# The first bias of the routed experts moves from a matmul into a row of the weights, with two raw buffers, fewer waits between the adds and 24 result slots

## What is computed

```python
x = x + tanh(g_xattn[0]) * xattn(_layernorm(x), ctx_1024, ctx_1024, Wq, bq, Wk, bk, Wv, bv, Wo, bo)
x = x + tanh(g_ffn[0]) * ffn(_layernorm(x), gate_w, gate_b, sw1, sb1, sw2, sb2, rw1, rb1, rw2, rb2)

def ffn(x, ...):                      # D = 256, FFN = 256, 8 experts, 1 shared, top 2
    hs = einsum('bsd,ndf->nbsf', x, sw1) + sb1[:, None, None, :]
    shared_out = einsum('nbsf,nfd->bsd', swiglu(hs), sw2) + sb2.sum(0)
    probs = softmax(x @ gate_w + gate_b, axis=-1)
    topk_probs, topk_idx = top_k(probs, 2)
    cw = sum(one_hot(topk_idx, 8) * topk_probs[..., None], axis=2)
    hr = einsum('bsd,edf->ebsf', x, rw1) + rb1[:, None, None, :]
    out_e = einsum('ebsf,efd->ebsd', swiglu(hr), rw2) + rb2[:, None, None, :]
    return shared_out + einsum('ebsd,bse->bsd', out_e, cw)
```

## Time and profile before

| | |
|---|---|
| runs | 696.72, 694.03, 694.46 us |
| median | 694.46 us |
| the profiled execution | 697.65 us |
| its span | 695.8 us |
| PE busy | 635.5 us (91%) |
| DVE busy | 482.7 us (69%) |
| ACT busy | 424.3 us (61%) |
| POOL busy | 230.7 us (33%) |
| mean granted clock of PE | 0.969 |

### The profile page before, as it was taken

The page is one execution under the profiler, slowest core; times in us unless marked ns, Lnnn a source line. Parts: engine busy times, 40 slices in busy tenths (PEclk is TensorE's granted clock), DMA queues, the critical chain, the costliest instruction groups (busy, mean ns, idle before and its releaser), DMA issues.

```text
span 695.8 us, 12724 instructions
## 1 busy us (share of the span) xinstructions
PE 635.5 (91%) x3603; PEld 332.6 (48%) x3616; DVE 482.7 (69%) x805; ACT 424.3 (61%) x842; POOL 230.7 (33%) x243
## 2 busy tenths in 40 slices
PE   3997687999999999999999999999988989999990
PEld 3776561223333333333333333345456778888870
DVE  4785879778888888888888888847777844444430
ACT  4674344777777777777777777766734224444440
POOL 2343324303431442244100211220057804555552
PEclk9998897999999999999999999999999999999995
DMA  7999697964697689767843660224079665655445
GB/s 238 333 270 310 222 233 176 154 97 95 143 192 197 187 157 186 193 172 153 163 62 61 90 106 32 92 75 168 24 266 312 231 184 87 102 98 96 73 47 143
DMA packets 82820, 108.22 MB, mean 156 GB/s; under 512 B 16553, under 2 KB 64563, under 8 KB 81814
## 3 DMA queue, kind: packets, MB, share of 16 engines
q1 hardware_dynamic: 71912, 78.58, 49.0%
q0 software_dynamic: 10864, 29.10, 15.8%
HBM read 62.10 MB, written 47.35 MB: 157 GB/s over the span
## 4 chain that ended last, share of the span: by engine, by line
PE 65%; issue 13%; POOL 6%; DVE 6%; DMA 5%; SPq 2%; ACT 1%; POOLq 1%; ACTq 0%; DVEq 0%
PE psS L1492 16%; PE psO L1519 16%; PE psM L1474 14%; PE psH L1737 8%; PE psY L1763 3%; POOL zs L720 3%; DMA kq<-k_parts 2%; DVE mneg L1125 1%; PE psO L1416 1%; DVE mneg L1049 1%; PE psX L1725 1%; PE psH L1748 1%; DMA acc<-ysb,ids 1%; PE psF L1446 1%; POOL parts L614 1%
## 5 line engine op out<-in xcount | busy, mean ns | idle before, releaser
L1125 DVE TENSOR_REDUCE mneg<-psM 128x1 f32<-128x1024 f32 x240 | 282.6, 1219 | 60.7 <-PE psM L1474 60.7
L859 ACT ACTIVATE pr<-psS 128x512 f32<-128x512 f32 x488 | 266.7, 595 | 94.8 <-PE psS L1492 94.8
L1492 PE MATMUL psS<-kq 99*128 99x512 bf16 x488 | 152.4, 385 | 2.1 <-DMA kq<-msb 1.5
L1519 PE MATMUL psO<-pr,vt 128*32 128x512 f32 x1024 | 136.4, 605 | 0.0
L1474 PE MATMUL psM<-kq 96*128 96x512 bf16 x480 | 127.3, 386 | 4.8 <-DVE mneg L1125 3.1
L1492 PEld LDWEIGHTS psS<-kq 99*128 99x128 bf16 x488 | 39.8, 97 | 149.6 <-ACT pr L859 131.3
L766 POOL DMA_INDIRECT acc<-ysb,ids x39 | 60.2, 1543 | 66.9 <-ACT ysb L982 32.1
L600 POOL TENSOR_TENSOR msb<-mcp,none 16x128 bf16<-16x128 f32 x16 | 6.2, 389 | 224.7 <-ACT mcp L836 224.7
L1474 PEld LDWEIGHTS psM<-kq 96*128 96x128 bf16 x480 | 46.2, 98 | 63.4 <-DVE mneg L1125 9.1
L1737 PE MATMUL psH<-wall,zgT 128*128 x234 | 68.2, 427 | 0.9 <-DVE zgT L1357 0.9
L1363 DVE TENSOR_TENSOR rg<-psH,rs 128x256 f32<-128x256 f32 x39 | 16.5, 424 | 66.4 <-ACT rs L970 66.4
(11 more groups left out here) (246 smaller groups left out, 828.5 us busy)
## 6 DMA issues: line engine op xcount, KB each, us to landing
kq<-k_parts SPq DMA_DIRECT2D x96, 128.0 KB, 5.7
w_parts<-wraw POOLq DMA_DIRECT2D x14, 768.0 KB, 4.3
wall<-w_parts SPq DMA_DIRECT2D x7, 1536.0 KB, 7.8
v_pad<-vst SPq DMA_DIRECT2D x16, 512.0 KB, 8.7
vt<-v_pad SPq DMA_DIRECT2D x16, 512.0 KB, 7.9
wraw<-wexp POOLq DMA_DIRECT2D x9, 768.0 KB, 7.6
k_parts<-parts SPq DMA_DIRECT2D x16, 384.0 KB, 6.7
kq<-q_parts SPq DMA_DIRECT2D x96, 64.0 KB, 5.3
```

Source lines behind the costliest of these rows:

```text
L859: nc.scalar.activation(pr[:, slot, j], score_bank(s, j), ACT.Exp, scale=SCALE).then_inc(e_done, 1)
L1125: V.tensor_reduce(mneg[:, parity, i:i + 1], psM[:, i % 2], X_AXIS, ALU.max, negate=True).then_inc(m_free, 1)
L1492: mm(score_bank(s, j), kst[:, slot, j, kt * P:(kt + 1) * P], qst[:, slot, j], start=True, stop=True).then_inc(s_full, 1)
L1519: last = mm(psO[j * VW:(j + 1) * VW, u % 2], vt[:, u, k, j * VW:(j + 1) * VW], pr[:, k % 4, j], start=(k == 0), stop=(k == KT - 1), skip_g ...
```

## The change

The change uses that a normalised row has the sum 0. The last number of a row is minus the sum of the others, so from each row of `w1` the last row can be subtracted and the last number of the row is then free. POOL writes 1.0 there before the scatter, and the last row of `w1` is replaced by the expert's first bias.

- **PE:** `tile_first` has six matmuls in place of seven. `brow1`, its clearing on POOL and its two loads on SP are gone, and so are the three parts of the first bias: SP stores the bias once, as fp32 rows (`b1_rows`), and POOL cuts only the second bias into parts.
- **POOL in attention:** `last_row_in` loads the last row of `w1` into all partitions of `aT` (a broadcast of 512 numbers). `less_last_row` starts the load of the bias into partition 127, subtracts the last row from both halves of `w1` (128 x 512, and 127 x 512), and waits for that load. This is done for seven late experts and the last routed one, 8 times in all.
- **Two raw buffers:** the raw weights of the late experts lie in `wraw[:, 0]` and the new `raw2` by turns. `raw_in(e + 1)` now comes at the end of `stage(e)`; the wait for the stores is in front of the cast.
- **POOL in the scatter:** a memset of 128 x 4 numbers and a wait ahead of each of the four batches.
- **Adds:** no wait at every sixth add; only the first of an expert's run waits. `ysb` has 24 slots, and ACT waits, from tile 24 on, for the issue of the add 8 before its own. DVE's table loses one instruction (L1290), POOL two iotas.

```diff
@@ -61,9 +61,8 @@
 TILES_R = NB * NQ * 2 // P + NR - 1
 TAB = 40
 ZG = 11
-YB = 12
-DRAIN = 6
-LAST_DRAIN = 30
+YB = 24
+RUN = NQ * NB // P
 WCOLS = DT * 2 * FF + DT * D
 BLK = 512
 EPS = 1e-5
...
@@ -144,9 +142,12 @@
         sZ = ExitStack()
         ysb = sb("ysb", [P, YB, D], F32, sZ)
         sb("shift", [P, QT * D + 2 * 2 * DT * BLK + DT * D + DT * BLK - YB * D + 4], F32, sZ)
-        brow1 = sb("brow1", [P, NE, 2 * D], BF16, sZ)
         brow2 = sb("brow2", [P, NE, D], BF16, sZ)
         sZ.close()
+        sR = ExitStack()
+        sb("raw_shift", [P, QT * D], F32, sR)
+        raw2 = sb("raw2", [P, WCOLS], F32, sR)
+        sR.close()
         a_in, zT0, wo_s, aT, zT1, zT2, zx012, pt, small, cmp, rank, chosen, before, held, uone, slf, slot_f, slot_u, nt2, tok, spare = (
             sb(*a) for a in z_names)
...
@@ -479,9 +481,10 @@
                 sp.wait_ge(o_taken, 4 * b + u + 2)
                 sp.dma_start(attn[b, :, :, u * HG * DH:(u + 1) * HG * DH], ast[:, u % 2]).then_inc(a_st[u % 2], 16)
-            sp.wait_ge(bp_ok, 2)
+            sp.wait_ge(bt_ok, 1)
+            sp.dma_start(b1_rows.rearrange("e (m p) -> (e m) p", p=P), b1_t[:]).then_inc(b1_st, 16)
+            sp.wait_ge(bp_ok, 1)
             for s in range(3):
-                sp.dma_start(b1_parts[s].rearrange("(q p) -> q p", p=P), b1_p[:, s]).then_inc(bp_st, 16)
                 sp.dma_start(b2_parts[s].rearrange("(e d) -> e d", d=D), b2_p[:, s]).then_inc(bp_st, 16)
             with sp.Fori(0, NB - 1) as b:
...
@@ -537,10 +540,7 @@
                     sp.dma_start(zs[bass.ds(row, P)], fill).then_inc(fill_st, 16)
             store_base(0)
-            sp.wait_ge(brow_ok, 2)
-            b1_rows = b1_parts.rearrange("s (e c) -> s e c", e=NE)
-            sp.dma_start(brow1[0:3, 0:NR], b1_rows[:, 1:NE]).then_inc(brow_ld, 16)
-            sp.dma_start(brow1[0:3, NR:NE], b1_rows[:, 0:1]).then_inc(brow_ld, 16)
+            sp.wait_ge(brow_ok, 1)
             sp.dma_start(brow2[0:3], b2_parts.rearrange("s (e c) -> s e c", e=NE)).then_inc(brow_ld, 16)
             store_base(1)
...
@@ -668,6 +666,28 @@
                                         ALU.add).then_inc(xb_ok, 1)
+            def raw_at(e):
+                return raw2[:] if e % 2 else wraw[:, 0]
+            def last_row_at(nth):
+                return aT[:, nth % 2]
+            def last_row_in(nth, e):
+                nc.gpsimd.dma_start(last_row_at(nth), wexp[raw_of(e), P - 1:P, 2 * FF:4 * FF].to_broadcast([P, 2 * FF])).then_inc(last_ld, 16)
+            def less_last_row(nth, e, raw):
+                if nth == 0:
+                    pool.wait_ge(b1_st, 16)
+                nc.gpsimd.dma_start(raw[P - 1:P, 2 * FF:4 * FF], b1_rows[raw_of(e):raw_of(e) + 1]).then_inc(b1_ld, 16)
+                pool.wait_ge(last_ld, 16 * (nth + 1))
+                nc.gpsimd.tensor_tensor(raw[:, 0:2 * FF], raw[:, 0:2 * FF], last_row_at(nth), ALU.subtract).then_inc(less_ok, 1)
+                nc.gpsimd.tensor_tensor(raw[0:P - 1, 2 * FF:4 * FF], raw[0:P - 1, 2 * FF:4 * FF], last_row_at(nth)[0:P - 1],
+                                        ALU.subtract).then_inc(less_ok, 1)
+                pool.wait_ge(less_ok, 2 * nth + 2)
+                pool.wait_ge(b1_ld, 16 * (nth + 1))
             def prepare(nth, e, r):
                 hi, lo = (wall[:, w_at(e) + 12 * part:w_at(e) + 12 * (part + 1)].rearrange("p u c -> p (u c)")
@@ -679,24 +699,29 @@
             def stage(e):
+                raw, hi = raw_at(e), wraw[:, 1]
                 pool.wait_ge(raw_ld[0], 16 * (2 + e))
-                nc.gpsimd.tensor_copy(wraw[:, 1].bitcast(F32R), wraw[:, 0]).then_inc(wp_hi, 1)
+                less_last_row(1 + e, e, raw)
+                if e:
+                    pool.wait_ge(wp_st, 32 * e)
+                nc.gpsimd.tensor_copy(hi.bitcast(F32R), raw).then_inc(wp_hi, 1)
                 pool.wait_ge(wp_hi, e + 1)
-                nc.gpsimd.tensor_tensor(wraw[:, 0].bitcast(F32R), wraw[:, 0], wraw[:, 1], ALU.subtract).then_inc(wp_ok, 1)
+                nc.gpsimd.tensor_tensor(raw.bitcast(F32R), raw, hi, ALU.subtract).then_inc(wp_ok, 1)
                 pool.wait_ge(wp_ok, e + 1)
-                nc.gpsimd.dma_start(w_parts[e, :, 0:WCOLS], wraw[:, 1]).then_inc(wp_st, 16)
-                nc.gpsimd.dma_start(w_parts[e, :, WCOLS:2 * WCOLS], wraw[:, 0]).then_inc(wp_st, 16)
+                nc.gpsimd.dma_start(w_parts[e, :, 0:WCOLS], hi).then_inc(wp_st, 16)
+                nc.gpsimd.dma_start(w_parts[e, :, WCOLS:2 * WCOLS], raw).then_inc(wp_st, 16)
+                if e + 1 < LATE:
+                    raw_in(e + 1)
             def raw_in(e):
-                pool.wait_ge(wp_st, 32 * e)
-                nc.gpsimd.dma_start(wraw[:, 0], wexp[raw_of(e)]).then_inc(raw_ld[0], 16)
+                nc.gpsimd.dma_start(raw_at(e), wexp[raw_of(e)]).then_inc(raw_ld[0], 16)
+                last_row_in(1 + e, e)
             for n in range(UNITS - 1):
                 if n >= UNITS - NG:
                     bias_x(n - UNITS + NG)
-                if 3 <= n < 2 + LATE:
-                    raw_in(n - 2)
                 split_max(n + 1, (n + 1) % 2)
                 if n == EARLY:
                     load_tail()
@@ -705,6 +730,10 @@
                 if n < EARLY:
                     pool.wait_ge(raw_ld[n], 16)
+                    if n == 0:
+                        last_row_in(0, NE - 2)
+                    else:
+                        less_last_row(0, NE - 2, wraw[:, 1])
                     prepare(n, NE - 1 - n, n)
                     if n == 1:
                         raw_in(0)
@@ -715,6 +744,8 @@
             def scatter(b):
                 pool.wait_ge(sl_ok, b + 1)
+                nc.gpsimd.memset(zx(b)[:, :, D - 1:D], 1.0).then_inc(ones_z, 1)
+                pool.wait_ge(ones_z, b + 1)
                 for k in range(2):
                     for t in range(QT):
                         nc.gpsimd.indirect_dma_start(
@@ -738,16 +769,13 @@
             nc.gpsimd.iota(row_i[:, 0:16], pattern=[[P, 16]], base=0, channel_multiplier=0).then_inc(io_c, 1)
             nc.gpsimd.iota(row_i[:, 16:16 + TAB], pattern=[[1, TAB]], base=0, channel_multiplier=0).then_inc(io_c, 1)
             nc.gpsimd.iota(row_i[:, 16 + TAB:64], pattern=[[REGION, NR]], base=0, channel_multiplier=0).then_inc(io_c, 1)
-            nc.gpsimd.iota(row_i[:, 64:64 + LAST_DRAIN + DRAIN], pattern=[[DRAIN, LAST_DRAIN // DRAIN + 1], [0, DRAIN]], base=0, channel_multiplier=0).then_inc(io_c, 1)
-            nc.gpsimd.iota(row_i[:, 64 + LAST_DRAIN + DRAIN:], pattern=[[0, TAB + 2 - LAST_DRAIN - DRAIN]], base=LAST_DRAIN, channel_multiplier=0).then_inc(io_c, 1)
-            pool.wait_ge(io_c, 9)
+            pool.wait_ge(io_c, 7)
             nc.gpsimd.tensor_copy(rowc[:], row_i).then_inc(u_ok, 1)
             scatter(2)
             scatter(3)
             pool.wait_ge(h_full, 6)
             pool.wait_ge(sc_done, 16 * 2 * QT * (NB - 1))
-            nc.gpsimd.memset(brow1[:].rearrange("p e c -> p (e c)").bitcast(F32), 0.0).then_inc(brow_ok, 1)
             nc.gpsimd.memset(brow2[:].rearrange("p e c -> p (e c)").bitcast(F32), 0.0).then_inc(brow_ok, 1)
             pool.wait_ge(base_st, 16 * NB)
@@ -757,12 +785,7 @@
                     waits = add_waits(mybir.EngineType.Pool, T_WAIT + i, 4)
                 pool.wait_ge(ry_ok, i + 1)
                 pool.wait_ge(id_ok, i + 1)
-                if i % DRAIN == 0 and i <= LAST_DRAIN:
-
-                    pool.wait_ge(added, 16 * (i + 1))
-                else:
-
-                    pool.wait_ge(added, waits[i % 4])
+                pool.wait_ge(added, waits[i % 4])
                 nc.gpsimd.indirect_dma_start(
                     out=acc[:, :], out_offset=bass.IndirectOffsetOnAxis(ap=ids[:, i:i + 1], axis=0),
                     in_=ysb[:, i % YB], in_offset=None, bounds_check=NB * NQ + (1 + SPARES) * P - 1, compute_op=ALU.add,
@@ -978,7 +1001,7 @@
                 act.wait_ge(ry_full, i + 1)
                 if i >= YB:
-                    act.wait_ge(issued, DRAIN * ((i - DRAIN) // DRAIN) + 1)
+                    act.wait_ge(issued, i - YB + RUN + 1)
                 nc.scalar.activation(ysb[:, i % YB], psQ[:, i % 2, 0:D], ACT.Identity,
                                      scale=zg[:, i % ZG, bass.ds(e + D, 1)]).then_inc(ry_ok, 1)
...
@@ -1287,7 +1310,6 @@
                 V.scalar_tensor_tensor(out=tab[:, T_W:T_W + TAB], in0=e_f, scalar=float(WU), in1=at,
                                        op0=ALU.mult, op1=ALU.add).then_inc(tab_ok, 1)
                 link(V.scalar_tensor_tensor(out=gone, in0=e_f, scalar=NR - 0.5, in1=gone, op0=ALU.is_lt, op1=ALU.mult))
-                link(V.tensor_tensor(gone, gone, drained, ALU.max))
                 V.tensor_scalar(tab[:, T_WAIT:T_WAIT + TAB], gone, 1.0, 16.0, ALU.add, ALU.mult).then_inc(tab_ok, 1)
             beside_attention = {1: ((r_sum, 0), (r_scale, 0)), 3: ((r_sum, 1), (r_scale, 1)), 5: ((r_sum, 2),), 6: ((r_low, 0), (r_scale, 2)),
```

(5 more changed lines are left out.)

34 lines of the change are left out of this document (16 added, 18 removed).

## The result

| | kernel before | kernel after |
|---|---|---|
| runs | 696.72, 694.03, 694.46, 690.95 us | 710.17, 712.44, 716.19, 706.86 us |
| median | 694.25 us | 711.31 us |
| the profiled execution | 697.65 us | 710.17 us |
| its span | 695.8 us | 708.3 us |
| mean granted clock of PE | 0.969 | 0.956 |

The ratio is 1.022, its 95% interval 1.0148 to 1.0292. The forecast was 685.4 us, in a range of 683 to 689.5. The change made the kernel 1.5 to 2.9% slower.

A forecast was written before the change was run, and what follows sets the result against it. PE's matmuls were taken to bound attention units and the tile stage. The terms -8.5 (bias matmul) + 0 (adds) + 0 (POOL in attention) - 0.6 (before first tile) = -9.1 us gave a median of 685.4 us, range 683 to 689.5.

The forecast's parts named there:

- POOL in attention: Staging of late experts: new subtractions, DMA issues and wait take 5.2 of POOL's 14.8 us idle per unit; cost 0.
- Rival D: Attention: split_max comes late in seven staging units because POOL waits for a landing, PE stops; 698 us, chance 0.05.
- The matmul of the bias: Tile stage: removing one 512-column matmul per tile gives 0.235 us each, 8.5 us over 36 first layers.
- Rival A: Tile stage: the first fp32 weight load shows, leaving 0.145 us gained per tile; median 688.6 us, chance 0.10.
- Adds and slots: Tile stage: dropping waits between adds, with 24 slots, gives 0 itself but avoids the last add being at least 2.3 us late.
- rival C: Tile stage: POOL's adds set the pace, run starts cost more than 4.69 us; 2 or 3 us back, median 688, chance 0.05.
- Between scatter and first tile: Stretch before the tiles: a 2.04 us memset goes, four small ones with waits come at 0.3 each; net -0.6 us.
- Rival B: Scatter: batches wait far longer than 0.3 us for memsets or land late, tile stage begins late; 689.0 us, chance 0.07.

The follow-up runs named there:

- the repeated pair: Kernel before and kernel after run again unchanged, each with its own new profile: 695.57 us (one run) and 711.15 us, ratio 1.0206.
- e4: Kernel before without the first-bias matmul in each tile, keeping the old waits at every sixth add and 12 slots: 706.02 us, ratio 0.9937 to the kernel before.
- e1: Kernel after with the last row of w1 loaded into one partition instead of broadcast to 128: 709.04 us, ratio 0.9999 to the kernel before.
- the first job: First of three batches of follow-up runs, holding e1, e2, e3 and e4; the kernel before had a median of 708.8 us in it.
- e3: Kernel after without last row, bias row, subtractions and their waits; two raw buffers and new tile stage stay: 693.09 us, ratio 0.9782 to the kernel before.
- e2: Kernel after without the load of the bias row and POOL's wait for it: 698.95 us, ratio 0.9846 to the kernel before.

## Why the prediction was wrong

**The step that failed** is "POOL in attention", with its "Cost 0; its upper end is 0 as well unless a DMA takes 10 us longer". It cost 24 us (26.6 in the repeated pair, where 2.8 are unit 2's). The step counted POOL's idle time, and there it was right: the new work fits, and POOL still waits 9.0 to 13.7 us for the maxima in each staging unit. It left out, without a reason, what the moved and added DMAs do to the transfers of the other engines: POOL's stores, 1.5 MB a unit, moved from 7.1 to 14.7 us of a unit in the stretched ones, ahead of twelve SP loads in whose queue a critical 4 KB transfer stands last. That transfer then landed 7.1 us after its issue in place of 1.9, and PE stood still. The window of the earlier trace rows had the sign, a DMA share of 0.79 with 180 GB/s moved, and I read only its engine columns.

**A size in the same step.** The bias row's landing was put at up to 4.1 us by the scatters of the earlier trace rows, covered for 2.6 by the subtractions. It took 7.2 to 7.7 us in five of the seven late experts (3.0 and 4.0 in the other two) and left POOL 4.55 us of waiting in the unit shown. A row of 2 KB is no smaller a wait than a large transfer when the DMA engines have a backlog. The Trainium skill (DMA: Bandwidth & Descriptors, Queues, rings and completion order) says that a DMA engine takes turns between queues, a packet at a time. By that rule the row should have passed SP's loads, since POOL's queue was empty when it was issued: the broadcast before it landed at 242.39 + 11.2 = 253.6, the row was issued at 255.50. This trace does not agree: the row landed after 7.5 us, and from 252 to 261.4 no packet of POOL's queue moved. The trace shows when packets move and not when they are ready to, so why the row stood is open.

**Rival D** named the right place, seven staging units in which PE stops, and the wrong late thing. It watched `split_max`, which was on time (its last step is at 227.37 in the chain above, and POOL had waited for ACT before it), while the 4 KB DMA behind it landed late. PE stopped in five of the seven. Its price per unit, that each us beyond the point is paid seven times, misses the clock: behind a stall of 2.5 us the granted clock fell to 0.50, and the unit paid 4.1.

**The matmul of the bias** was right in its mechanism. The period is 2.639 us where 2.643 was predicted. From first to 34th add PE's pace gave 95.0 - 87.0 = 7.9 us, in the repeated pair too. Predicted were 8.5 by 36 tiles; it is 33 periods of 0.239, since the first add comes no sooner behind the first turn (9.8 us before, 9.7 to 10.8 after). Rival A is out with the period. The Trainium skill (TensorE: Matmul & The Clock Gate, Back-to-back issue gap) has about 131 ns as the sustained spacing of 512-column matmuls. The trace does not agree: the matmul removed was worth 239 ns here.

**Adds and slots.** Right: in POOL's last adds, which answer to the earlier trace rows, only run starts wait for a landing, and the end behind the 34th is nearly unchanged (28.0 us, before 27.6). The profile names ACT for the second wait, but this tile's result was there at 682.1, and 684.95 - 680.27 = 4.68 us is the time of a landing as in the earlier trace rows:

```profile
680.27 1.54 POOL L789 DMA_INDIRECT acc<-ysb,ids  x1 [1.10 <-ACT ysb L1005]
684.95 1.54 POOL L789 DMA_INDIRECT acc<-ysb,ids  x1 [3.15 <-ACT ysb L1005]
...
691.32 1.54 POOL L789 DMA_INDIRECT acc<-ysb,ids  x1 [2.98 <-DMA acc<-ysb,ids]
...
695.01 1.54 POOL L789 DMA_INDIRECT acc<-ysb,ids  x1 [0.30 <-issue]
```

Its size was small: the old waits would have cost 6.3 us by e4 (its 34th add is at 103.1 behind the first turn, with the new waits at 96.8), where at least 2.3 was given. Of rival C the mechanism is there and the price is not: the run start at the 20th add took 5.3 us in one profile of the kernel after and 6.3 in the other, not 4.69, and POOL had caught up by the 34th in both.

**Between scatter and first tile.** Predicted -0.6; the profiles have +0.6 and, in the repeated pair, -1.7. Among runs that differ this much it can't be told. The memset that was put at 0.3 with its wait took 0.13 us at its longest. The third of the four, and the DMA behind it:

```profile
552.42 0.09 POOL L747 MEMSET zx<- 128x4 f32 x1
553.33 1.05 POOL L751 DMA_INDIRECT zs<-zx,slot_u  x1 [0.81 <-POOL zx L747]
```

The wait behind it is the 0.81, so one costs 0.9 us in place of 0.3. Rival B's place was right so far, but no late start of the tile stage can be told from it.

## What to carry to other kernels

When DMAs are added or moved, ask which small transfer stands on the critical path and what the DMA engines still hold when it is issued. An engine's idle time says nothing about that; the DMA share of each microsecond around that issue does. In this kernel it helped to put the bulk stores early in a period, to wait for them, and to let nothing large stand ahead of the next critical load: the same work in one order made it 15 to 17 us slower than before, in another 10 us faster. And a stall can cost more than its own length once the granted clock falls behind it.

## What the runs showed of the hardware

- After a stall of 2.52 us PE's granted clock was 0.50 for 3.4 us, and the unit with this stall took 4.1 us longer, not 2.5. In e1 three units with stalls of 1.3 to 1.8 us kept a clock of 1.00 and took 1.5 to 2.0 us longer.
- SP's loads of queries and keys moved 98 to 139 GB/s with the DMA engines full (slices 4 to 17 below; 290 and 279 in the next two), where POOL's stores moved 315 to 462. The share is nearly the same in both; the GB/s tell them apart. The kernel after from 250 to 275 us, in 40 slices (busy tenths, then GB/s; the stores begin in the 32nd):

```profile
DMA  9999999999999999999600000000000798999988
GB/s 174 205 239 103 98 134 136 125 121 125 133 130 130 117 115 107 139 290 279 126 0 0 0 0 0 0 0 0 0 0 0 315 462 324 374 413 256 206 187 359
```

- In the first job, in the profiles of e1, e3 and e4, ACT waited 9.3 to 11.5 us and DVE 3.5 to 8.5 behind attention for something that no engine of the core released. From e4:

```profile
530.05 1.28 DVE L1173 SCALAR_TENSOR_TENSOR xs<-psY,tg,xs 128x1024 f32<-128x1024 f32 x1 [8.49 <-remote]
530.18 1.26 ACT L921 ACTIVATE g<-psH,b_s 128x512 f32<-128x512 f32 x2 [9.34 <-remote]
```

The stretch between attention and the tiles took 60 to 66 us there, against 54 to 56 in the other jobs and in the profiles of before and after (58 in e2). That goes with the slower kernel before of that job. Its cause wasn't tested and stays open.
